# Angle parts and the position counter move from VectorE to GpSimd

## The reference

```python
omega_scale = jnp.exp(omega_log_scale)                                 # one per head and mode
angles = pos[:, None, None, None] * omega_scale[None, :, :, None] * inv_freq
cos = jnp.transpose(jnp.cos(angles), (2, 0, 1, 3))
...
qr = _l2norm(_rotary(q, cos, sin)) * scale
kr = _l2norm(_rotary(k, cos, sin))
...
S = S * jnp.exp(b_g)[..., None, None]                                  # fade
dv = (v_t[None] - einsum(k_t, S)) * b_beta[..., None]
S = S + k_t[..., :, None] * dv[..., None, :];  o_t = einsum(q_t, S)
o = jnp.einsum('tmbhv,hm->bthv', ys, mode_w)                           # mode weights
```

## Time and profile before

| | |
|---|---|
| median of 3 runs | 6816.04 us (6806.51 to 6821.66) |
| profiled execution | 6782.06 us, span 6780.4 us |
| mean granted TensorE clock | 0.822 |
| DVE busy | 5129.9 us (76%) |
| PE busy | 4499.9 us (66%) |
| ACT busy | 3431.5 us (51%) |
| POOL busy | 2767.9 us (41%) |

### The profile page before, as it was taken

The page is one execution under the profiler, slowest core; times in us unless marked ns, Lnnn a source line. Parts: engine busy times, 40 slices in busy tenths (PEclk is TensorE's granted clock), DMA queues, the critical chain, the costliest instruction groups (busy, mean ns, idle before and its releaser), DMA issues. The chain is left out here.

```text
span 6780.4 us, 195918 instructions
## 1 busy us (share of the span) xinstructions
PE 4499.9 (66%) x78513; PEld 3871.6 (57%) x78513; DVE 5129.9 (76%) x9800; ACT 3431.5 (51%) x6010; POOL 2767.9 (41%) x1789
## 2 busy tenths in 40 slices
PE   1666666667666666666667666676666666655993
PEld 1556655556655656655566555566555665553662
DVE  4888888888888888888888888888888888881003
ACT  1555555555555555555555555555555555542220
POOL 3444343444343444443444444443434444433003
PEclk6788888888878888888888878788788888877996
DMA  2000000000000000000000000000000000013123
GB/s 91 2 6 6 6 5 6 6 5 3 5 5 5 6 6 6 6 5 6 5 5 3 5 5 6 5 6 6 5 6 5 6 3 5 5 35 110 61 69 108
DMA packets 77480, 109.71 MB, mean 16 GB/s; under 512 B 20577, under 2 KB 66209, under 8 KB 75425
## 3 DMA queue, kind: packets, MB, share of 16 engines
q1 hardware_dynamic: 67616, 71.42, 3.3%
q0 software_dynamic: 8960, 25.39, 1.2%
HBM read 57.89 MB, written 38.89 MB: 14 GB/s over the span
## 5 line engine op out<-in xcount | busy, mean ns | idle before, releaser
L1573 POOL TENSOR_TENSOR state<-state,gc_end 128x512 f32<-128x512 f32 x512 | 592.2, 1174 | 1626.7 <-PE bank L595 1586.2
L572 PE MATMUL bank<-state,ke 128*64 128x64 f32 x16384 | 641.4, 246 | 310.2 <-DVE outT L1309 169.4
L572 PEld LDWEIGHTS bank<-state,ke 128*64 128x64 f32 x16384 | 607.9, 159 | 379.8 <-issue 189.7
L608 PE MATMUL last_two<-dvs,kte 128*64 128x64 f32 x16384 | 691.8, 248 | 180.3 <-DVE dvs L1298 180.2
L589 PE MATMUL bank<-rhs,te 128*64 128x64 f32 x8192 | 408.0, 252 | 521.4 <-DVE rhs L1291 284.5
L847 ACT ACTIVATE ke<-kq 32x512 f32<-32x512 f32 x1024 | 643.0, 628 | 201.4 <-DVE kq L1223 187.7
L1272 DVE TENSOR_TENSOR last_two<-last_two,prod 128x31 f32<-128x31 f32 (+15 forms) x1984 | 693.0, 349 | 68.1
L608 PEld LDWEIGHTS last_two<-dvs,kte 128*64 128x64 f32 x16384 | 629.5, 161 | 196.6 <-DVE dvs L1298 187.3
L1270 DVE TENSOR_TENSOR prod<-bd,last_two 128x31 f32<-128x31 f32 (+15 forms) x1984 | 670.4, 338 | 68.3
L797 ACT ACTIVATE te<-tt 32x256 f32<-32x256 f32 x1024 | 421.9, 412 | 565.1 <-DVE tt L1275 554.5
L589 PEld LDWEIGHTS bank<-rhs,te 128*64 128x64 f32 x8192 | 341.1, 161 | 599.3 <-DVE rhs L1291 550.6
(11 more groups left out here) (257 smaller groups left out, 10393.1 us busy)
## 6 DMA issues: line engine op xcount, KB each, us to landing
w_sb<-in_L_ffn_W_dram SPq DMA_DIRECT2D x16, 1024.0 KB, 9.4
expert_rows<-ke SPq DMA_DIRECT2D x1, 8192.0 KB, 21.9
xrows<-expert_rows SPq DMA_DIRECT2D x16, 512.0 KB, 8.5
expert_outputs<-yrow POOLq DMA_DIRECT2D x16, 512.0 KB, 3.4
xt<-_attn_hidden_states_dram SPq DMA_DIRECT2D x32, 128.0 KB, 2.8
xr<-_attn_hidden_states_dram SPq DMA_DIRECT2D x32, 128.0 KB, 2.1
x_after_attention<-xr SPq DMA_DIRECT2D x32, 128.0 KB, 1.7
xo<-x_after_attention SPq DMA_DIRECT2D x32, 128.0 KB, 3.7
```

The lines of the kernel that those rows point to most:

```text
L572: mm = pe.matmul(bank_mem[g][s, q % 4 * DK:q % 4 * DK + DK], ke[:, c, r, q, s], state[:, hh * HQ + q, r, :], start=(r == 0), stop=(r == 1))
L608: mm = pe.matmul(bank_upd[g][s, (q % 4) * P + r * DK:(q % 4) * P + r * DK + DK], kte[:, r, q, s], dvs[:, q, :], start=True, stop=True)
L1573: pool.tensor_tensor(sv, sv, gc_end[:, vh, 4 * g:4 * g + 4, c].unsqueeze(2).broadcast_to([P, 4, 2 * DK]), ALU.mult).then_inc(sem(f"state_f ...
```

## The change

`angle_parts` and the advance of `pos` are taken off DVE. POOL gets a function of the same name with the same arithmetic. It is called in `half` behind the fade of chunk 3 and ahead of the wait for pw_raw, and once ahead of the first half. It waits for k_rotated (the keys' rotation reads the same buffer, tmp) where DVE waited for q_rotated; the semaphore parts_ready goes, since the reader is now on the same engine. V_STEPS and G_STEPS count the steps of DVE's and POOL's chains.

```diff
@@ vector
-                ln(dve.tensor_scalar(pos[:], pos[:], float(P), None, ALU.add))
@@
-            def angle_parts(n, hh, steps_, general=False):
...
-                if not last:
-                    angle_parts(n2, hh2, (0, 1), general=first)
                 chunk_systems(u, 1)
-                if not last:
-                    angle_parts(n2, hh2, (2, 3), general=first)
                 chunk_systems(u, 2)
...
-            angle_parts(0, 0, range(4), general=True)
             half(0, 0, first=True)
@@ gpsimd
+            def angle_parts(n, hh, general=False):
+
+                om = (omega[:] if general else tab[:, 0])[:, hh * HQ:hh * HQ + HQ].unsqueeze(2).broadcast_to([P, HQ, P])
+                if hh == 0:
+                    pool.sem_inc(sem("pool_held"), 1)
+                    ln(pool.tensor_scalar(pos[:], pos[:], float(P), None, ALU.add))
+                pool.wait_ge(sem("k_rotated"), since("k_rotated", 2 * n + hh))
+                if not general:
+                    pool.wait_ge(sem("tab_in"), 16 * n)
+                ln(pool.tensor_tensor(tm[0], pos[:].unsqueeze(1).broadcast_to([P, HQ, P]), om, ALU.mult))
+                pool.sem_inc(sem("pool_held"), 1)
+                ln(pool.tensor_scalar(tm[0], tm[0], inv_freq, None, ALU.mult))
+                grid = ROUND11 if general else ROUND12
+                pool.sem_inc(sem("pool_held"), 1)
+                ln(pool.tensor_scalar(tm[1], tm[0], grid, -grid, ALU.add, ALU.add))
+                ln(pool.tensor_tensor(tm[0], tm[0], tm[1], ALU.subtract))
+                if general:
+                    pool.sem_inc(sem("pool_held"), 1)
+                    ln(pool.tensor_scalar(tm[2], tm[0], ROUND23, -ROUND23, ALU.add, ALU.add))
+                    ln(pool.tensor_tensor(tm[0], tm[0], tm[2], ALU.subtract))
...
             def low_turns(n, hh, general=False):
-                pool.wait_ge(sem("parts_ready"), 2 * n + hh + 1)
                 ln(turns_part(hh, general, 1, low))
...
                 if not first:
                     fade(u - 1, 1 - hh, 3)
+                if not last:
+                    angle_parts(*after(n, hh), general=first)
 
                 pool.wait_ge(sem("pw_raw"), u + 1)
...
             group_rows(0)
+            angle_parts(0, 0, general=True)
             low_turns(0, 0, general=True)
```

More of the change, by code:

```diff
@@ L305, in build @@
         DVE_TURNS = (13, 26)
-        V_STEPS = (92, 185)
-        G_STEPS = (29, 26)
+        V_STEPS = (81, 178)
+        G_STEPS = (42, 35)
         def after(n, hh):
@@ L1396, in half @@
                 vh = 1 - hh
-                n2, hh2 = after(n, hh)
+                n2 = after(n, hh)[0]
                 def memories(step, c):
```

## The result

The changed kernel takes 6643.89 us (median of 4 runs, 6633.98 to 6649.09), the kernel before 6811.27 beside it: a ratio of 0.9755 [0.9737, 0.9773], where the forecast's factor was 0.977.

A forecast was written before the change was run, and what follows sets the result against it. DVE is busiest overall, but PE is fuller from gram 0 to the transpose and sets the pace after the change: 6782 - 172 + 12 + 7 = 6629, factor 0.977, by the median 6662 us, range 6612 to 6715.

The forecast's parts named there:

- The bound: Gram 0 to the solve's transpose: without the steps PE's queue sets the time, 15.87 us (hh = 0) and 13.62 (hh = 1).
- the cover of a tenth of a us: In hh = 1 halves DVE frees the first chunk's bank at about +10.3, while PE is on gram 2 until +10.44.
- Removed from DVE: Angle steps, 3.90 us per half, and the counter, 0.23 per pair: 249 us of DVE time, some 258 with gaps.
- What of it reaches the end: Gram 0 to the transpose gets shorter by 2.30 us (hh = 0) and 3.26 (hh = 1), 172 us together.
- rival B: Slow gram 3 pieces from PE's clock persist and every scan waits 2 us: gain halved, about 6729 us, chance 0.11.
- POOL's price: Steps behind POOL's last fade take 6.8 us (7.1 with pos), at most 9.3 and 9.7, hidden in POOL's idle time.
- both signs: POOL's steps ending 4 us or more ahead of L1598 would show it right, its scalar rows above 3.3 us wrong.
- Rival D: POOL's scalar form takes 6 us or more, so the steps never leave the path: 6816 within 15, chance 0.04.
- Collisions in the stretch: DVE work beside POOL's new steps has a PSUM operand or reads one tensor, so blocking was priced at nothing.
- rival C: POOL's hold on the shared port also blocks DVE products with one SBUF operand: slower, about 7080 us, chance 0.05.
- The scan: L1144 beside POOL's turn sums waits longer: +0.4 us a pair, bounds -1.4 and +1.2, +12 us in all.
- The start: First tile's six steps on POOL ahead of its turn sums: +10.2 us, first half gains about 3.2, net +7.

The follow-up runs named there:

- half_gram_after: The changed kernel with half of each gram's products left out (output wrong): 6501.58 us, ratio 0.9584 to the kernel before.
- half_gram_before: The kernel before with half of each gram's products left out (output wrong): 6758.1 us, ratio 0.9966 to the kernel before.
- before_again: The kernel before, unaltered, run once more for a second profile: 6799.16 us in total.
- no_parts: The changed kernel with POOL's angle steps and position counter left out in the loop (angles wrong): 6652.09 us, ratio 0.9771 to the kernel before.
- pool_plus1: The changed kernel with the rounding done twice on POOL in the loop, same output: 6580.09 us, ratio 0.970 to the kernel before.
- pool_plus3: The changed kernel with the rounding done four times on POOL in the loop, same output: 6851.43 us, ratio 1.01 to the kernel before.
- split_round: The changed kernel with the first parts back on DVE and the rounding split into two one-immediate tensor_scalars on POOL: 6626.99 us, one run.
- best2: The changed kernel with first parts on DVE, POOL's frequency product two-input, clipping two solve steps earlier, scan one later: 6566.78 us, ratio 0.9683 to the kernel before.
- ahead_of_fade: The changed kernel with POOL's angle steps ahead of the last fade instead of behind it: 7095.62 us, one run.

## Why the prediction was right, and where its terms were off

- **The bound.** Right. Gram 0 to the transpose was forecast at 15.87 and 13.62 us and is 15.93 and 13.51 on average. half_gram_after shows that PE now sets the stretch (it fell by 2.6 and 1.8 us with shorter grams); half_gram_before, that DVE did so behind gram 0 before (hh = 1 fell by 1.15, hh = 0 by an estimated 0.8 once L625's lower clock is taken off). In hh = 1 halves the three grams take 5.89 us, not 5.80: the cover of a tenth of a us was about used up.
- **Removed from DVE.** 249 to 258 us forecast for 62 halves, 263.7 measured on the page for the whole kernel, which holds the longer first two rounds of steps too. The half-gram kernels' 257 us is no second measurement of it (see there).
- **What of it reaches the end.** Forecast -5.56 us a pair, measured -5.85: -2.23 for -2.30 and -3.62 for -3.26. The second was sized from one half of 16.88 us, while the mean was 17.13: the mean also holds the halves with a slow gram 3. Before, gram 3 took 2.6 to 3.6 us in 20 of the 31 hh = 1 halves (12 in before_again), at a granted clock of 0.54 in the one of the earlier trace rows; after, all 62 pieces of three grams take 5.8 to 5.9 us (L533 in all: 542.6 us before, 512.7 after). That is rival B turned round: the lower clock came with the waits, and went with them. This part of the gain was not forecast.
- **POOL's price.** This term failed as priced. I took 1.1 us for a tensor_scalar with 2.36 as the upper bound; they take 2.85 and 3.65, so the chain is 11.2 us in hh = 0 (2717.62 to 2728.85) and 12.0 in hh = 1 instead of 6.8 and 7.1. The text called rows above 3.3 us a sign that it is wrong, and steps that end 4 us ahead of the weights a sign that it is right; both signs speak against it (3.65 us; 2.6 ahead with hh = 0, 0.6 too late with hh = 1). It still cost nothing (no_parts). With hh = 0 the cover was long enough; with hh = 1 that is luck, since the weights have slack behind the transpose, at least 4.5 us there and 3.8 with hh = 0, that I had not counted. The Trainium skill, in the GPSIMD Engine Reference (Engine selection), has one-input elementwise work on GpSimd at roughly line rate; here it is slower than the two-input form, 2.85 and 3.65 against 2.36 us, so the trace disagrees.
- **Rival D** put the point of no change at tensor_scalars of 6 us, a chain of 16.6 us. pool_plus1's is 15.1 and 15.9 us (11.2 and 12.0, and 3.9 more), and the kernel is 3% ahead; in hh = 0 halves it is free up to about 11.2 + 2.6 + 3.8 = 17.6. With 11.5 us more (pool_plus3) the kernel is 1% behind, so the point of no change lies between the two, and beyond D's: the 1.5 us from 15.1 to 16.6 can cost at most 62 x 1.5 = 93 of the 200 us gained.
- **Collisions in the stretch.** Right: L1235 takes 425 ns (L1256 424 before), L1286 692 (L1307 691), the statistics L1131 428 as before. The operations with a PSUM operand run beside POOL undisturbed for 12 us a half; rival C falls.
- **The scan.** Forecast +0.4 us a pair; it fell by 0.5 to 1.26, and the clipping, which I had not looked at, rose by 0.4 (0.41 to 0.83). Together -0.08 us; between the second profiles of the two kernels (0.50+1.44 and 0.77+1.33) it is +0.16, so no sign can be read from it. That they matter was right, and the size of the matter was about 1 us a pair either way (pool_plus1, split_round, best2). The clipping reads one SBUF tensor and a scalar and is held all the same (1.70 us beside L1541 instead of 0.28): "two SBUF operands", on which the collision part rested, is too narrow. The rule in SBUF — State Buffer (SBUF: two separate sides) of the Trainium skill names 2-port modes beside two inputs, and has the lock held for the whole instruction. The trace can't show the mode, but it agrees with that wider form: the clippings ended 76 to 83 ns behind POOL's operation.
- **The start.** Forecast +10.2 less 3.2, measured +14.1: DVE's first L1148 comes at 171.21, against 154.44 for the first L1169 of before, +16.8, since three of the six steps are tensor_scalars that take 10.1 us together and not 3.3. DVE's row in the kernel before:

```profile
154.44 0.69 DVE L1169 TENSOR_SCALAR cos_t<-tmp 128x1024 f32<-128x1024 f32 x1 [22.41 <-POOL tmp L1538]
```

POOL's and DVE's timelines at the start of the changed one:

```profile
132.06 1.89 POOL L1510 TENSOR_TENSOR tmp<-pos,omega 128x1024 f32<-128x1024 f32 x1
...
134.16 2.85 POOL L1512 TENSOR_SCALAR tmp<-tmp,cmat 128x1024 f32<-128x1024 f32 x1 [0.21 <-POOL tmp L1510]
...
137.21 3.64 POOL L1515 TENSOR_SCALAR tmp<-tmp 128x1024 f32<-128x1024 f32 x1 [0.19 <-POOL tmp L1512]
...
143.47 3.63 POOL L1519 TENSOR_SCALAR tmp<-tmp 128x1024 f32<-128x1024 f32 x1 [0.20 <-POOL tmp L1516]
...
171.21 0.69 DVE L1148 TENSOR_SCALAR cos_t<-tmp 128x1024 f32<-128x1024 f32 x1 [45.77 <-POOL tmp L1533]
```

- **The sum.** Forecast -172 + 12 + 7 = -153; measured -183 + 14 = -169 (the tail left out), 0.9751 of the profiled 6782, and the timed ratio is 0.9755. The errors are -9 for the stretch, -14 for scan and clipping and +7 for the start, and partly cancel; to that extent the closeness is luck. With before_again's loop the measured sum is -161.

## What to carry to other kernels

Work taken from the busiest engine pays only until the next one fills the stretch: read how long that engine runs where nothing holds it (here the last half), and take the difference, not the work removed. A move onto an idle engine is free as long as it delays nothing there beyond the slack of those that wait for it: 11.6 us a half cost nothing behind the fade and 481 us in all ahead of it. Then look at the short operations of the other engine that the new one holds up: moving two of them by one or two solve steps was worth 35 us, a fifth of the whole change.

## What the runs showed of the hardware that was not expected

- On POOL a tensor_scalar of 128x1024 fp32 takes 2.85 us with a scalar per partition, 2.77 with one immediate and 3.65 with two; tensor_tensor takes 2.36, and 1.90 with a spread operand. Two operations in one instruction are cheaper than two instructions (3.65 against 5.54), and a product with a per-partition scalar is cheaper as a two-input one.
- The clipping and the scan, DVE operations of 0.28 and 0.42 us without a PSUM operand, are held until just behind the end of a POOL operation that runs when they start (by 76 to 83 ns and by 273 to 282 ns), and last up to 2.44 and 2.61 us (pool_plus1, ahead_of_fade). L1235 and L1286, with a PSUM operand, keep their 0.42 and 0.69 us.
- After PE waits of 3.00 and 1.65 us, and of 5.17 us, the next matmuls ran at a granted clock of 0.50: such an idle stretch cost about 1.8 us beside its own length (3.78 for 1.99, and 3.68 for 1.93, a third of 5.80). The length of the one wait doesn't settle it: in half_gram_before some grams took their 1.15 us at a granted clock of 0.97 to 1.00 after 4.22 us, others 1.98 at 0.50.
- The tail of one and the same kernel took 737 or 763 us, and 766 or 740. Over the experiments it went with the chip: 761 to 765 us with 15 to 19 "remote" waits on one, 737 to 741 with none on the other.
